# Fewer source columns picked by TensorE, more gathered by GpSimd, in the GAT passes of a graph network

## The chip, the cores and the metric

The kernel runs on one NeuronCore of a Trainium2 chip. The metric is device time in microseconds. The kernel before takes 10527.93 us, the median of 3 runs (10525.65 to 10530.43).

## The reference

A graph of 6250 nodes with 64 features and 100000 edges, sorted by destination, goes through four networks, each followed by a residual and a layer norm. What matters here is the second, a graph attention network (GAT) of five layers with one set of edges:

```python
h = x @ W
al = h @ a_src
ar = h @ a_dst
logit = leaky_relu(al[src] + ar[dst], 0.2)
alpha = segment_softmax(logit, dst)
out = segment_sum(alpha[:, None] * h[src], dst) + b
```

Four layers use W_std, then one uses W_skip on the concatenation of input and result. The first network sums rows by edge with a sigmoid weight, the third is again an attention with k[src] · q[dst] (in the kernel "dot"), the fourth has three layers with four heads ("multi").

## The kernel before, in words

The 100000 edges, padded, lie as 128 partitions × 784 columns, cut into CHUNKS = 28 chunks of K = 28 columns. A chunk is processed as a unit: the table rows of its 28 × 128 source nodes must stand in `rows[:, b]` (two buffers, b = chunk mod 2; the trace calls this memory `turned`), then DVE and ACT compute logits, running maxima and exponentials, DVE multiplies the rows with the weights (L1426) and scans them into sums by destination (L1446), and ACT turns the result (L1084, L1086) and stores it.

There are two ways to get a column of source rows (128 rows of 66 floats in GAT):

- **Gathered.** POOL issues one indirect DMA per column (L970). `gather` waits first for `rows_used[b]`, which DVE's L1426 of two chunks earlier signals.
- **Picked.** PE multiplies one-hot matrices with the table of all nodes, which is held on chip in `pair`, split in two parts of float32r. A column takes 7 sets × 2 parts = 14 matmuls of 462 columns (L1115). ACT makes the one-hots from keys (L733, L744), SP loads the keys. DVE takes each picked column out of its PSUM bank with a mask (L1236, `take`), and one reduction for half of the columns writes the rows (L1240).

`Picks.X` says how many of the 28 columns are picked: `COLS["gat"]` = 8 in four of the GAT edge passes and `FIRST_COLS` = 7 in the first; `KG = K - X` are gathered. EARLY = X // 2 columns of a chunk are taken ahead of the previous chunk's L1426, the rest after its scans. In the four passes with `ahead=2` the first chunk has further 2 × X columns picked, so that `gather(0, 0, KG - X * AH)` is short. The picked columns' PSUM banks form a ring of RING = 6 (`bank_of`).

Each engine runs its own program, and hardware loops (`Fori`) go over pairs of chunks; only semaphores order them, so the order is written out by hand. `layer` (L1891) does a node part (`nodes`) and the edge part (`edges`). `build` calls it once for the sum network with the first GAT edges, three times in a `Fori` for the standard layers, once for the last standard layer with W_skip edges, once for dot, and for the multi layers. PICKED = max(COLS.values()) sets how many key columns `prepare` computes and stores, and KEYS and KEY_TURNS follow from it.

The dot pass picks 4 of 28 columns with other code (L1128, L1222, L1227); the multi passes pick none.

Of the kernel before, what the change touches and what calls it, by code (L numbers as in the profile page):

```python
# [45 lines left out]
class Link:  # L46


    def __init__(self, eng, sem, base=0):
        self.eng, self.sem, self.base, self.n = eng, sem, base, 0  # L50
# [607 lines left out]
NG = 7  # L658
GC = C // NG
GROUPS = [(j * GC, (j + 1) * GC) for j in range(NG)]  # L660
COLS = {"gat": 8, "dot": 4}
FIRST_COLS = 7
PICKED = max(COLS.values())
HALF = D
KF = 2 * D
# [12 lines left out]
def edge_tiles(kind, update=False, clear=None, **_):  # L678

    X = COLS.get(kind, 0)  # L680
    multi_kind = kind == "multi"
# [18 lines left out]
class Picks:  # L700


    def __init__(self, nc, g, ph, kind, ahead, cols=None):
        X = self.X = cols or COLS[kind]
        self.ahead, self.first = ahead, AHEAD - ahead
# [1185 lines left out]
def layer(nc, g, node, edge=None):  # L1891

    with phase(nc) as ph:
        turned, rows = ph.shared("turned", *[f for f, _ in (node_tiles(**node), edge_tiles(**edge) if edge else ({}, {}))])
        wide, chunk = ph.shared("wide", *[f for _, f in (node_tiles(**node), edge_tiles(**edge) if edge else ({}, {}))])
        banks = ph.psum("banks", [P, 8, 512])[:]
        ph.now = ph.block()
        pk = Picks(nc, g, ph, edge["kind"], edge["ahead"], edge.get("cols")) if edge and edge["kind"] in COLS else None
        ready = nodes(nc, g, ph, banks, turned, wide, pk=pk, **node)
        if edge:  # L1900
            edges(nc, g, ph, banks, rows, chunk, ready, pk=pk, **edge)
# [6 lines left out]
def build(nc, a, out):  # L1908
    g = Graph()
    with ExitStack() as ctx:  # L1910
# [38 lines left out]
        with scratch(nc, "proj", [P, C, D + 2]) as proj:  # L1949
          g.proj = proj  # L1950
          with scratch(nc, "pair", [P, 2, SETS, D + 2, SET], F32R) as pair:
# [3 lines left out]
            std = dict(gat, weights=g.gat_w[0:D, 1, :])  # L1955
            layer(nc, g, dict(kind="sum", rows=g.x, w_o=a["l0_w"], **std), dict(kind="gat", ahead=0, cols=FIRST_COLS))
            with nc.Fori(0, 3):
# [86 lines left out]
```

## Time and profile before

| | us |
|---|---|
| timed, median of 3 runs | 10527.93 |
| profiled execution, its span | 14084.2 |
| gather loop of the first GAT pass | 1033.7 |
| gather loops of the four others | 1113.3, 1117.2, 1110.9, 1115.5 |
| gather loop of dot | 1220.1 |
| gather loops of multi | 1170.7, 1293.9, 1294.1 |
| POOL busy, DVE busy, PE busy | 7724.8, 7042.7, 6814.7 |

The profiled execution is one execution of the same program with the hardware profiler on; for it only the span is known, from the first to the last instruction, and no other time of its own. It is a third longer than the timed runs. In the tables of the profile PE is TensorE's matmuls, PEld its weight loads, DVE VectorE, ACT ScalarE, POOL GpSimd, SP SyncE. A "gather loop" is the stretch from the first to the last L970 of a layer. PEclk is the granted TensorE clock as a share of 2.4 GHz, so 0.50 is 1.2 GHz. "Issue" as the end of an idle time means that nothing shown in the profile was waited for.

### The profile page before, as it was taken

Reading aid. Unit: us, or ns where it says so; the run is one execution under the profiler, and the core shown is the slowest. Engines: PE = TensorE matmul, PEld = TensorE weight load, DVE = VectorE, ACT = ScalarE, POOL = GpSimd, SP = SyncE. Lnnn points to the kernel's source line nnn. Section 1 sums busy time; section 2 is a strip of 40 time slices with the busy share of each in tenths; the row PEclk is TensorE's granted clock in tenths of the full one; section 3 lists DMA queues with packets and bytes.
Section 4 is the critical chain, followed back from the end, with each engine's and each line's share of the span. In section 5 each row is a group of like instructions: output and inputs, shape, how many; then the busy total and the mean of one; then the engine's idle time right before and its main releaser. Section 6 shows DMA issues by size and latency. Waiting matters only on the chain. (4 is left out here: it accounts for less than half of the span.)

```text
span 14084.2 us, 100376 instructions
## 1 busy us (share of the span) xinstructions
PE 6814.7 (48%) x27637; PEld 5669.8 (40%) x27637; DVE 7042.7 (50%) x12322; ACT 5152.3 (37%) x5609; POOL 7724.8 (55%) x7576
## 2 busy tenths in 40 slices
PE   5443366657756774777577646661111322232222
PEld 5433355545545553655455535551111211121111
DVE  5333345434444443444444546663444466646666
ACT  0011144444434443444344424442222243423432
POOL 7888755544444445344444455546665555545553
PEclk7555577768777776887677767775555565556555
DMA  5333322212211221122133323333332344434442
GB/s 154 36 36 33 58 51 58 56 39 55 54 49 42 56 55 42 48 55 55 40 90 91 86 72 97 97 89 89 115 109 96 116 143 136 140 94 141 138 140 81
DMA packets 782270, 1137.56 MB, mean 81 GB/s; under 512 B 500471, under 2 KB 559955, under 8 KB 774499
## 3 DMA queue, kind: packets, MB, share of 16 engines
q0 software_dynamic: 355008, 370.44, 14.1%
q1 hardware_dynamic: 363245, 417.03, 9.6%
q10 hardware_dynamic: 63926, 349.09, 6.2%
q8 instruction: 32, 0.52, 0.0%
q14 instruction: 59, 0.48, 0.0%
HBM read 680.14 MB, written 468.70 MB: 82 GB/s over the span
## 5 line engine op out<-in xcount | busy, mean ns | idle before, releaser
L970 POOL DMA_INDIRECT turned<-d_t,idx x5788 | 5465.9, 944 | 5006.3 <-DVE wide L1426 3228.1
L1115 PE MATMUL banks<-pair,hot 128*128 128x462 f32 x16184 | 3981.1, 402 | 1677.0 <-issue 1661.2
L1115 PEld LDWEIGHTS banks<-pair,hot 128*128 128x128 f32 x16184 | 3357.4, 208 | 2299.7 <-issue 1921.1
L1236 DVE TENSOR_TENSOR wide<-banks,member 128x462 f32<-128x462 f32 x1156 | 689.9, 634 | 2788.3 <-remote 2123.6
L1084 ACT COPY wide<-wide 128x952 f32<-128x952 f32 (+2 forms) x252 | 503.4, 1997 | 2831.5 <-DVE wide L1446 2800.7
L650 POOL DMA_INDIRECT d_acc<-work,idx x784 | 1237.7, 1579 | 263.9 <-issue 234.4
L733 ACT ACTIVATE hot<-keys,row 128x1024 fp32r<-128x1024 f32 (+1 forms) x1036 | 1073.1, 1117 | 277.9 <-PE banks L1115 204.9
L1171 PE MATMUL banks<-ident,wide 128*128 128x128 f32 x588 | 163.1, 423 | 1814.2 <-issue 945.2
L1446 DVE TENSOR_TENSOR_SCAN wide<-banks,wide 128x224 f32<-128x224 f32 (+4 forms) x1288 | 1036.9, 871 | 5.8
L1128 PE MATMUL banks<-pair,hot 128*128 128x448 f32 x3136 | 804.7, 417 | 452.1 <-issue 393.8
L1128 PEld LDWEIGHTS banks<-pair,hot 128*128 128x128 f32 x3136 | 688.1, 221 | 568.7 <-issue 492.5
L744 ACT ACTIVATE hot<-hot 128x3584 fp32r<-128x3584 f32 (+1 forms) x296 | 905.2, 3105 | 0.6
L1171 PEld LDWEIGHTS banks<-ident,wide 128*128 128x128 f32 x588 | 103.5, 212 | 1881.9 <-issue 973.3
L1426 DVE TENSOR_TENSOR wide<-turned,banks 128x1792 f32<-128x1792 f32 x252 | 858.5, 3407 | 0.0
L1180 PE MATMUL banks<-wide,ident 128*128 128x512 f32 x224 | 199.5, 1026 | 1219.3 <-DVE wide L1319 1219.3
L1240 DVE TENSOR_REDUCE turned<-wide 128x264 f32<-128x1848 f32 (+1 forms) x296 | 601.6, 2033 | 10.1
L1180 PEld LDWEIGHTS banks<-wide,ident 128*128 128x128 f32 x224 | 63.0, 312 | 1303.0 <-issue 1303.0
L579 PE MATMUL banks<-ident,key_f 128*128 128x128 f32 x1568 | 248.9, 332 | 676.1 <-DVE key_f L528 645.1
L1294 DVE TENSOR_TENSOR_SCAN banks<-banks,wide 128x224 f32<-128x224 f32 x896 | 512.6, 618 | 117.7 <-DMA wide<-d_acc 70.4
L1086 ACT COPY wide<-wide 128x896 f32<-128x896 f32 (+2 forms) x252 | 521.2, 2068 | 48.3 <-remote 26.8
L1406 DVE SCALAR_TENSOR_TENSOR logits<-logits,we_rows 128x112 f32<-128x112 f32 x84 | 30.1, 358 | 1010.6 <-ACT we_rows L1000 944.6
L579 PEld LDWEIGHTS banks<-ident,key_f 128*128 128x128 f32 x1568 | 238.9, 240 | 685.6 <-DVE key_f L528 649.8
(311 smaller groups left out, 9556.1 us busy)
## 6 DMA issues: line engine op xcount, KB each, us to landing
d_e<-wide ACTq DMA_DIRECT2D x168, 924.0 KB
turned<-d_t,idx POOLq DMA_INDIRECT x5788
d_e<-wide ACTq DMA_DIRECT2D x84, 1008.0 KB
wide<-d_b SPq DMA_DIRECT2D x60, 1344.0 KB
keys<-d_key SPq DMA_DIRECT2D x124, 512.0 KB
d_b<-wide SPq DMA_DIRECT2D x28, 1344.0 KB
wide<-d_edge SPq DMA_DIRECT2D x84, 448.0 KB
d_em<-wide ACTq DMA_DIRECT2D x84, 448.0 KB
```

The source lines that it names most:

```text
L650: gp.indirect_dma_start(g.d_acc[r][:, :], offset(idx[:, b, k:k + 1]), sums[:, b, k, :], None, compute_op=ALU.add).then_inc(added[b][r], 16)
L733: last = nc.scalar.activation(pk.hot[:, place, :, j, :], pk.keys[:], ACT.Abs, bias=g.row[:, j * SET:j * SET + 1], scale=-1.0)
L744: last = nc.scalar.activation(part, part, ACT.Relu, bias=1.0, scale=-1.0)
L970: gp.indirect_dma_start(rows[:, b, k, :], None, table[:, :], offset(idx[:, b, k:k + 1])).then_inc(s["gathered"][b], 16)
L1086: nc.scalar.copy(state[:, :, FA:], values[:, b, FA:, :].rearrange("p f k -> p k f")).then_inc(s["states_turned"], 1)
L1115: mm = nc.tensor.matmul(ps_cols[i], hot[:, place, i, j, :], flat(g.pair[:, part, j]), start=(j, part) == (0, 0), stop=(j, part) == (SETS - ...
L1128: mm = nc.tensor.matmul(ps_cols[i][:, h], hot[:, i // 2, i % 2, j, :], flat(pk.pair[:, part, j, h * HALF:(h + 1) * HALF, :]), start=(j, pa ...
L1236: nc.vector.tensor_tensor(found[:, i - i0], ps_cols[i].rearrange("p (w c) -> p w c", c=SET), mid(member[:, i], TW), ALU.mult).then_inc(pic ...
L1240: link(nc.vector.tensor_reduce(rows[:, buf, at + i0:at + i1, :], found[:, 0:i1 - i0], AX.X, ALU.add))
L1294: last = nc.vector.tensor_tensor_scan(ps_q[:, f0 * K:(f0 + MR) * K], ps_same[:, 0:MR * K], flat(b_f[:, b, i * HEAD_ROWS + f0:i * HEAD_ROWS ...
L1426: nc.vector.tensor_tensor(V[:, 0:D, :].rearrange("p (h d) k -> p h d k", h=H), G[:, :, v0:v0 + D].rearrange("p k (h d) -> p h d k", h=H), ...
L1446: last = nc.vector.tensor_tensor_scan(flat(V[:, f0:f1, :]), flat(keep[:, m:m + f1 - f0, :]), flat(V[:, f0:f1, :]), 0.0, ALU.mult, ALU.add)
```

## The change

In the GAT passes TensorE picks 4 columns of a chunk in place of 8 (in the first pass in place of 7), and GpSimd gathers 24 in place of 20 (in place of 21). PICKED becomes 4, and everything that is derived from X follows.

```diff
-COLS = {"gat": 8, "dot": 4}
-FIRST_COLS = 7
+COLS = {"gat": 4, "dot": 4}
+FIRST_COLS = 4
 PICKED = max(COLS.values())
```

POOL in a layer with `ahead=2` (L1886 is the last DMA of the node part, the first L970 row the two gathers ahead of the loop, the second the loop body of two chunks):

```order
 L1886 DMA seed<-d_t,dst 128x66
 L961 UNCONDITIONAL_BRANCH
-L970 DMA turned<-d_t,idx 128x66 x24
+L970 DMA turned<-d_t,idx 128x66 x40
 L976 UNCONDITIONAL_BRANCH
 L976 ISA
-L970 DMA turned<-d_t,idx 128x66 x40
+L970 DMA turned<-d_t,idx 128x66 x48
 L976 REGISTER_ALU
```

Ahead of the loop 40 gathers stand in place of 24, and 48 in place of 40 in each pass of the loop.

DVE inside the loop, in the row that follows the logits (ISA rows are waits), where the early columns of the next chunk are taken ahead of L1425 and L1426:

```order
 L1232 ISA
-L1232 TENSOR_TENSOR member<-iota,in_set 128x56
-L55 REGISTER_ALU
-L1235 REGISTER_ALU
-L1236 TENSOR_TENSOR wide<-banks,member 128x462
...
-L1240 TENSOR_REDUCE turned<-wide 128x264
+L1232 TENSOR_TENSOR member<-iota,in_set 128x28
+L55 REGISTER_ALU
+L1235 REGISTER_ALU
+L1236 TENSOR_TENSOR wide<-banks,member 128x462
...
+L1240 TENSOR_REDUCE turned<-wide 128x132
 L55 REGISTER_ALU
```

Four takes and a reduction of 4 columns become two takes and a reduction of 2; the late columns change in the same way.

## Rows read from the trace of the kernel before

**Rows 1.** The page: span and instructions, busy time of each engine.
```profile
span 14084.2 us, 100376 instructions
PE 6814.7 (48%) x27637; PEld 5669.8 (40%) x27637; DVE 7042.7 (50%) x12322; ACT 5152.3 (37%) x5609; POOL 7724.8 (55%) x7576
```
**Rows 2.** Waits: who waited for whom: us in total, times, longest.
```profile
POOL turned L970 <- DVE wide L1426: 3228.1, 216, 83.1
DVE wide L1236 <- remote: 2123.6, 189, 37.1
...
DVE logits L1406 <- ACT we_rows L1000: 944.6, 74, 21.9
...
DVE wide L1236 <- PE banks L1115: 448.5, 199, 17.5
...
DVE proj L1222 <- remote: 315.6, 29, 46.1
```
**Rows 3.** Windows, gather loops: length, PE, PEld, DVE, ACT, POOL busy, PEclk, DMA, GB/s.
```profile
1774.90:2808.60 1033.70, 680.11 (x2708) 567.01 (x2708) 480.18 (x805) 467.68 (x419) 555.06 (x588) 0.78 0.22 56
2994.50:4107.80 1113.30, 792.41 (x3242) 669.52 (x3241) 527.50 (x851) 525.72 (x429) 513.43 (x544) 0.80 0.20 53
...
8240.20:9460.30 1220.10, 776.08 (x3021) 662.70 (x3020) 745.23 (x1123) 498.71 (x631) 634.44 (x672) 0.77 0.36 94
9657.70:10828.40 1170.70, 131.91 (x571) 122.61 (x571) 544.27 (x1143) 330.01 (x514) 740.22 (x784) 0.53 0.34 111
11050.60:12344.50 1293.90, 337.91 (x891) 204.46 (x891) 818.54 (x1522) 515.59 (x661) 741.08 (x784) 0.60 0.43 140
...
sum 10469.40, PE 5436.02 PEld 4442.23 DVE 5519.76 ACT 4428.77 POOL 5465.69; mean PE 604.00 PEld 493.58 DVE 613.31 ACT 492.09 POOL 607.30
```
**Rows 4.** Timeline, POOL: start, length, instruction, idle before and releaser.
```profile
4298.59 0.96 POOL L970 DMA_INDIRECT turned<-d_t,idx  x1 [0.31 <-issue]
...
4411.35 0.94 POOL L970 DMA_INDIRECT turned<-d_t,idx  x1 [83.10 <-DVE wide L1426]
...
4723.99 0.94 POOL L970 DMA_INDIRECT turned<-d_t,idx  x1 [0.30 <-issue]
...
4763.48 0.94 POOL L970 DMA_INDIRECT turned<-d_t,idx  x1 [16.08 <-DVE wide L1426]
```
**Rows 5.** Timeline, PE in the same steady chunk.
```profile
4713.15 23.39 PE L1115 MATMUL banks<-pair,hot 128*128 128x462 f32 x99 [0.85 <-issue]
4739.13 0.54 PE L1115 MATMUL banks<-pair,hot 128*128 128x462 f32 x1 [2.59 <-issue]
```
**Rows 6.** Timeline, PE at the start of a standard layer's loop.
```profile
4284.98 13.52 PE L1115 MATMUL banks<-pair,hot 128*128 128x462 f32 x55 [2.98 <-issue]
...
4318.54 0.54 PE L1115 MATMUL banks<-pair,hot 128*128 128x462 f32 x1 [2.95 <-issue]
...
4334.64 85.55 PE L1115 MATMUL banks<-pair,hot 128*128 128x462 f32 x397 [0.15 <-issue]
```
**Rows 7.** Timeline, DVE during the long run of rows 6.
```profile
4351.28 0.64 DVE L1236 TENSOR_TENSOR wide<-banks,member 128x462 f32<-128x462 f32 x1 [2.19 <-PE banks L1115]
4354.22 0.64 DVE L1236 TENSOR_TENSOR wide<-banks,member 128x462 f32<-128x462 f32 x1 [2.29 <-PE banks L1115]
...
4357.82 2.08 DVE L1240 TENSOR_REDUCE turned<-wide 128x264 f32<-128x1848 f32 x1
```
**Rows 8.** Groups of instructions: POOL's indirect DMAs outside the gather loops.
```profile
L650 POOL DMA_INDIRECT d_acc<-work,idx x784 | 1237.7, 1579 | 263.9 <-issue 234.4 <-ACT work L620 25.5 <-DMA d_acc<-work,idx 4.0
...
L1876 POOL DMA_INDIRECT wide<-d_e,idx_last x441 | 424.1, 962 | 145.1 <-issue 131.6 <-DMA d_e<-merged,idx_join 13.4
...
L1883 POOL DMA_INDIRECT d_b<-proj,idx_first x245 | 251.6, 1027 | 160.6 <-ACT proj L1820 89.8 <-issue 70.8
...
L1883 POOL DMA_INDIRECT d_b<-wide,idx_first x196 | 195.2, 996 | 186.1 <-ACT wide L1820 91.9 <-issue 53.7 <-ACT wide L1818 40.5
```
**Rows 9.** Timeline, PE after the last gather (4107.8) of a standard layer.
```profile
4111.46 16.27 PE L1115 MATMUL banks<-pair,hot 128*128 128x462 f32 x71 [0.86 <-issue]
```
**Rows 10.** Windows, as rows 3: a stretch at the lower clock, and the steady chunk.
```profile
4713.50:4718.00 4.50, 4.50 (x13) 3.85 (x13) 3.42 (x4) 0.00 (x0) 0.00 (x0) 0.50 0.00 0
4722.74:4763.48 40.74, 28.86 (x120) 24.59 (x119) 19.18 (x32) 18.26 (x15) 18.87 (x20) 0.79 0.19 53
```

## The prediction

> **What bounds the kernel now.** I read the page first [rows 1]. POOL is the busiest engine (55%), but no engine is near full, so shares settle nothing. The waits come next [rows 2]: POOL's gathers wait 3228.1 us in 216 waits for DVE's L1426, the multiply that gives a buffer of rows back, and DVE waits 2123.6 + 448.5 us at L1236 for the picked columns. So in this execution the chain is PE, then DVE, then POOL. The windows of the nine gather loops [rows 3] give the sizes: a standard GAT loop takes about 1115 us, of which POOL is busy 513.
>
> One steady chunk shows why. POOL issues 20 gathers, one every 1.248 us (0.944 busy, 0.30 between) [rows 4], then idles 16.08 us. This chunk takes 40.74 us [rows 10], and the 20 gathers fill 25 of them. PE's rows of the same chunk [rows 5] come in two kinds: 99 matmuls in 23.39 us, then single ones 2 to 3 us apart, with "issue" as the reason, so nothing that the profile shows holds them. At the start of a loop the pattern is plainer [rows 6]: single matmuls while POOL gathers, and 397 in 85.55 us once POOL is silent. A column is 14 matmuls; DVE takes one every 2.93 us there [rows 7], so eight columns need 23.5 us of PE and not 37 to 40.
>
> **How the profiled execution stands to the timed runs.** Its span is 14084.2 us, the median 10527.93: 3556 us less. Nothing in the kernel differs between the two. The largest thing that could shrink by as much is POOL's waiting: without the 3228.1 us the span is 10856. I conclude that PE's thin stretches belong mostly to the profiled execution. Then the timed run sits near a balance: 20 gathers of price p against 23.5 us of PE.
>
> What is p outside the profile? It lies between 0.944 (the gap gone) and 1.248 (all as shown). A balance over the whole program narrows it. Outside the nine loops lie 14084.2 − 10469.4 = 3615 us; 1666 other indirect DMAs stand there [rows 8] and get cheaper by (1.248 − p) each; about 100 us are late picks after the last gather (picks go on for 20 us after a standard loop, [rows 9]) and the like. That leaves 1436 + 1666p. The loops: first layer 588p + 7 (POOL sets it, since 7 columns are 20.5 us); four standard loops of 685 (worked out below); the first multi loop 784p + 10; the two later ones 28 × 36.2 each, their 46.2 a chunk [rows 3] less some 10 of the 12.8 us that L1406 waits on average for a product of the thin PE [rows 2]; dot 28 × 32.3, its 43.6 a chunk less the 315.6 / 28 us that L1222 waits [rows 2, 3]. The sum is 7126 + 3038p = 10528, so **p = 1.12**. The 7126 may be wrong by 200 us, which is ±0.07.
>
> **The change, part by part** (28 chunks a layer; the skip layer is built as the three standard ones, so four loops count alike).
> - *POOL.* A standard loop issues 24 × 28 − 8 = 664 gathers in place of 20 × 28 − 16 = 544, the first layer 672 in place of 588: 564 more in all.
> - *PE.* 56 matmuls a chunk in place of 112 (98 in the first layer): 11.7 us at full clock in place of 23.5. It is no longer near any limit.
> - *ACT and DVE.* The one-hot rows (L733, L744) halve, and of DVE's work four of eight takes of 0.64 us and half of two reductions of 2.08 go [rows 7]. Both engines had room within 25 us (DVE 19.2 and ACT 18.3 us busy in that chunk, [rows 10]), so this is costed at nothing; the cover is POOL's gathers, and if they did not cover it, it could only gain.
> - *Key loads and setup.* Half as many key bytes, one turned key tile less: a few us, counted as nothing, hidden behind POOL's scatters.
> - *Start of a loop.* Chunk 0 has 16 columns picked ahead and 4 gathered now; then 8 and 16. POOL's second burst is behind L1426 of chunk 0, and that is behind 28 picked columns (three groups of 8 and the early 4 of the next). PE starts 13.6 us before the first gather (4284.98 against 4298.59 [rows 4, 6]); 28 × 2.93 = 82, so 68 us after it; with the last take, reduction and L1426 75 us (shown: 112.8, with the thin stretch in it). After the change it is 14 columns, 41 us, released at about 35, while POOL has 40 gathers (45 us) to do: no wait.
>
> **Sum for a standard loop.** Before: release 0 at 75, one chunk every 23.5 us, release 25 at 663, last burst 20p: last gather ends at 685, and the last picks and last chunk take 20 more: 705. After: POOL never waits: 664p + 8 (0.3 us at each chunk) + 14 for the last chunk. With p = 1.12 this is 766: **+61 each, +243 for four.** First layer: 84p = **+94**. Together +337 us: 10528 + 337 = **10865**.
>
> The bounds of p: at 0.944 the same sum is 4 × (649 − 705) + 79 = −145, so 10383; at 1.248 POOL already sets the pace before (20 × 1.248 + 0.3 = 25.3 a chunk, 746 a loop) and it is 4 × (851 − 746) + 105 = +525, so 11053.
>
> After the change PE works less than half of a chunk, so its clock matters. The rows: at the lower level (0.50) 4.5 us hold 12 whole matmuls, 0.38 each [rows 10]; the long start-up run is at the upper one, 0.2155 each [rows 6]; and the granted clock is lowest, 0.53, in the loop where PE works least, the first multi loop [rows 3]. 56 matmuls at 0.38 are 21 us, below the 26.9 of 24 gathers: no cost. The Trainium skill, "TensorE: Matmul & The Clock Gate", section "HAM oscillation — how this bites in real kernels", says that PE falls back to half rate when it idles between bursts, so that every burst starts slow. By that rule a start-up's 14 columns take 75 us, not 41, of which POOL's 40 gathers cover all but some 23: the sum would be +337 + 92 = +429. The rows show that burst at full clock after a dozen matmuls, so I keep +337.
>
> **The rivals.**
> - *POOL's price is the full 1.248.* For it: the gap of 0.30 between gathers [rows 4] recurs unchanged and looks like the engine's own. Against: then the timed runs must have lost over 400 us outside the loops that no row shows as idle. Time 11053. Its harshest form puts every added gather on the path, at each loop's start too: 564 × 1.248 = +704, 11232. Against that stand the 83.10 us that POOL waits there now [rows 4] and that shrink, so it gets 2 in 100 by itself. The Trainium skill, "Perfetto Trace Analysis", section "Identifying the Most-Contended Engine", has the rule behind it: relieve the engine with the highest occupancy first, and here that engine is given more.
> - *Faster: PE's thin stretches are partly real.* If the timed PE also loses time while POOL gathers, a chunk before is longer than 23.5 us, and the balance above lowers p to match. With p = 1.00 the balance leaves 365 us, 2.2 a chunk over the 168 picking chunks (28 in each of five GAT layers and dot): a standard loop was 763 and becomes 686, the first layer +84 − 60, together −284: 10244. It decides where the old loop's loss outweighs the dearer POOL: at p about 1.06, with 1.1 us lost a chunk. For it: the stretches follow POOL's bursts to within some us, as contention would. Against: to lose much, POOL must be much cheaper than shown, and its 0.944 of busy time is a floor.
> - *The two effects cancel* (p near 1.06): 10528.
> - That the change does not do what it says is ruled out by the order of the instructions.
>
> **How the numbers follow.** Forecast (p 1.07 to 1.19, PE clean): 0.54. Full price, its harshest form included: 0.19. Faster: 0.21. Cancelling: 0.06. A measurement here can tell 0.2% (21 us) from no change, so slower 0.73, same 0.06, faster 0.21. The time is the likeliest case's, 10865. The range runs from 10390 (the lower bound of p; it leaves out half of the faster rival) to 11055 (the upper bound).
>
> **What the changed profile would show.** L970 ×6352 in place of 5788; L1115 ×8288. In the GAT layers POOL's wait for L1426 all but gone, one unbroken row of gathers 1.248 apart, PEclk lower. Since those waits vanish, the *profiled* GAT loops get shorter (664 × 1.248 + 8 = 837 in place of about 1115, first layer 847 in place of 1033.7), and the profiled span falls by some 1200 to 1300 us although the timed median rises. Dot and multi loops unchanged. The forecast is wrong if the median falls with the span, or if POOL still waits in the standard loops.

## The result

The change takes 11179.81 us, the median of 4 runs (11175.43 to 11182.93), against 10528.74 for the kernel before (4 runs, 10525.65 to 10530.43). The ratio is 1.0617 (95% interval 1.0602 to 1.0632): slower by 651 us, 6.2%. Forecast were 10865 and a range up to 11055. The direction was right, and the loss is nearly twice the one forecast.

Quote of the page of the changed kernel, its span and busy times and two of its groups; they answer to [rows 1]:

```profile
span 11178.5 us, 83592 instructions
PE 4839.5 (43%) x19740; PEld 4043.7 (36%) x19740; DVE 6426.9 (57%) x11757; ACT 4316.5 (39%) x5609; POOL 8268.3 (74%) x8140
...
L970 POOL DMA_INDIRECT turned<-d_t,idx x6352 | 5999.7, 945 | 1945.7 <-issue 1930.5
L1115 PE MATMUL banks<-pair,hot 128*128 128x462 f32 x8288 | 2081.6, 417 | 2107.6 <-ACT hot L744 2033.9
```

The first thing to see is the span: 11178.5 us, 1.3 us below the timed median. The profile of before had a span of 14084.2 beside timed runs of 10528. This was taken for a property of the profiled execution; the experiments find it on two chips in timed runs too, so it is most likely one of the chip that the profile was taken on (no record says which one that was). POOL is now busy for 74% of the span, and the rest of its time at L970 is 1930.5 us in 6328 steps of 0.30 us with no one to wait for.

The waits of the changed kernel (who waited for whom: us in total, times, longest), to be read beside [rows 2]:

```profile
DVE idx L1356 <- DMA turned<-d_t,idx: 2454.3, 187, 27.0
PEld banks L1115 <- issue: 2085.4, 130, 16.7
PE banks L1115 <- ACT hot L744: 2033.9, 130, 16.3
POOL turned L970 <- issue: 1930.5, 6328, 0.7
```

POOL's wait for DVE's L1426 has fallen from 3228.1 to 15.2 us in all. DVE now waits for gathered rows (L1356), and PE for its one-hots, which come at the pace of the chunks. Everything is behind POOL.

Windows of the changed kernel (length, PE, PEld, DVE, ACT and POOL busy, PEclk, DMA share, GB/s): the gather loops of the first GAT pass, two standard layers, dot and two multi layers, beside [rows 3]:

```profile
1764.10:2602.80 838.70, 388.81 (x1557) 332.38 (x1555) 402.23 (x737) 349.07 (x416) 634.19 (x672) 0.73 0.28 67
2759.10:3587.90 828.80, 378.34 (x1484) 322.86 (x1484) 400.44 (x734) 344.34 (x411) 626.68 (x664) 0.72 0.29 67
3745.40:4574.20 828.80, 378.92 (x1484) 323.51 (x1484) 400.49 (x734) 344.38 (x411) 626.74 (x664) 0.72 0.29 67
6709.30:7558.20 848.90, 682.47 (x3034) 614.53 (x3033) 753.50 (x1134) 502.39 (x635) 634.39 (x672) 0.88 0.51 135
7733.10:8711.70 978.60, 133.40 (x588) 124.13 (x588) 555.88 (x1170) 339.42 (x532) 739.94 (x784) 0.55 0.42 135
8876.00:9856.80 980.80, 348.99 (x893) 206.16 (x894) 830.67 (x1544) 524.60 (x676) 742.21 (x784) 0.64 0.58 185
```

Divide a length by its number of gathers: 838.7 / 672 = 1.248, 828.8 / 664 = 1.248, 978.6 / 784 = 1.248, 980.8 / 784 = 1.251. POOL's rhythm is the length of every loop. The dot and multi loops, whose code the change does not touch, take 849, 979 and 981 us here and took 1220, 1171 and 1294 in [rows 3]. That alone says that the profile of before is not of the same kind of execution.

PE at the start of a standard loop and in a steady chunk of the changed kernel (start, length, instruction, idle before), beside [rows 5, 6]:

```profile
3695.91 44.31 PE L1115 MATMUL banks<-pair,hot 128*128 128x462 f32 x196 [3.02 <-DVE pair L767]
...
4102.41 14.63 PE L1115 MATMUL banks<-pair,hot 128*128 128x462 f32 x56 [15.67 <-ACT hot L744]
```

There are no single matmuls any more. The 14 columns of the start (196 matmuls) are done in 44.31 us, before POOL's first gather at 3745.37. PE starts 49.5 us ahead of that gather, and not 13.6 as in [rows 4, 6].

### The profile page after: what moved, and what is told of

Read it like the earlier page. It is cut to its first block and busy times, and to the rows that moved or that the text cites. A ratio compares the mean times of both kernels' runs of the same rounds, so it can differ in the third digit from the quotient of the medians.

```text
span 11178.5 us, 83592 instructions
## 1 busy us (share of the span) xinstructions
PE 4839.5 (43%) x19740; PEld 4043.7 (36%) x19740; DVE 6426.9 (57%) x11757; ACT 4316.5 (39%) x5609; POOL 8268.3 (74%) x8140
## 5 line engine op out<-in xcount | busy, mean ns | idle before, releaser
L970 POOL DMA_INDIRECT turned<-d_t,idx x6352 | 5999.7, 945 | 1945.7 <-issue 1930.5
L1115 PE MATMUL banks<-pair,hot 128*128 128x462 f32 x8288 | 2081.6, 417 | 2107.6 <-ACT hot L744 2033.9
L1115 PEld LDWEIGHTS banks<-pair,hot 128*128 128x128 f32 x8288 | 1782.1, 218 | 2406.0 <-issue 2085.4
L1356 DVE COPY idx<-src 128x28 int32 x252 | 47.1, 187 | 2459.7 <-DMA turned<-d_t,idx 2454.3
L1426 DVE TENSOR_TENSOR wide<-turned,banks 128x1792 f32<-128x1792 f32 x252 | 853.3, 3386 | 0.0
L1063 ACT ACTIVATE banks<-factors 128x28 f32<-128x28 f32 (+1 forms) x252 | 55.7, 221 | 1928.7 <-DVE factors L1416 1928.7
L1128 PE MATMUL banks<-pair,hot 128*128 128x448 f32 x3136 | 705.7, 390 | 171.2 <-ACT hot L759 166.4
L1128 PEld LDWEIGHTS banks<-pair,hot 128*128 128x128 f32 x3136 | 635.6, 204 | 241.4 <-issue 172.0
L733 ACT ACTIVATE hot<-keys,row 128x512 fp32r<-128x512 f32 x1036 | 651.4, 710 | 104.2 <-ACT wide L1086 43.2
L1876 POOL DMA_INDIRECT wide<-d_e,idx_last x441 | 438.0, 993 | 145.1 <-issue 131.6
L620 ACT COPY work<-banks 128x512 f32<-128x512 f32 x112 | 51.5, 546 | 1228.9 <-DMA d_acc<-work,idx 1217.3
L744 ACT ACTIVATE hot<-hot 128x1792 fp32r<-128x1792 f32 x296 | 483.9, 1681 | 0.6
L1017 ACT COPY wide<-wide 128x28 f32<-128x28 f32 (+2 forms) x240 | 418.1, 1742 | 159.1 <-DMA wide<-d_b 110.9
```

The lines of the kernel that those rows point to most:

```text
L733: last = nc.scalar.activation(pk.hot[:, place, :, j, :], pk.keys[:], ACT.Abs, bias=g.row[:, j * SET:j * SET + 1], scale=-1.0)
L744: last = nc.scalar.activation(part, part, ACT.Relu, bias=1.0, scale=-1.0)
L970: gp.indirect_dma_start(rows[:, b, k, :], None, table[:, :], offset(idx[:, b, k:k + 1])).then_inc(s["gathered"][b], 16)
L1115: mm = nc.tensor.matmul(ps_cols[i], hot[:, place, i, j, :], flat(g.pair[:, part, j]), start=(j, part) == (0, 0), stop=(j, part) == (SETS - ...
L1128: mm = nc.tensor.matmul(ps_cols[i][:, h], hot[:, i // 2, i % 2, j, :], flat(pk.pair[:, part, j, h * HALF:(h + 1) * HALF, :]), start=(j, pa ...
L1426: nc.vector.tensor_tensor(V[:, 0:D, :].rearrange("p (h d) k -> p h d k", h=H), G[:, :, v0:v0 + D].rearrange("p k (h d) -> p h d k", h=H), ...
```

## Experiments

Theories: **A**, POOL issues a gather every 1.248 us in timed runs too and paces every loop, the only other cost being a short wait at the start of each standard loop; **B**, the prediction's price of 1.12; **C**, the profiler stretches PE.

### The kernel before once more, and three parts of the change

e_before is the kernel before, unchanged.

> The kernel before, unchanged, profiled once more, since the changed kernel's profile spans no more than its timed runs. Theory A (POOL sets the pace in undisturbed runs, each gather costs the full 1.248 us, and the earlier profile was a disturbed execution): a span near 10528 us, gathers 1.248 us apart, PE without thin stretches, the four standard GAT gather loops near 690 us each and the last multi loops near 980 us as in the changed kernel. Theory B (the price of 1.12 from the prediction): gathers about 1.12 us apart, standard loops near 685 us. Theory C (the profiler always thins out PE in this kernel): a span near 14084 us again.

It took 10534.89 us, with a span of 10533.0. Its page, two windows (first pass, a standard loop) and two more (both kinds of multi loop):

```profile
span 10533.0 us, 100376 instructions
PE 6226.2 (59%) x27637; PEld 5319.9 (51%) x27637; DVE 7031.4 (67%) x12322; ACT 5148.8 (49%) x5609; POOL 7742.1 (74%) x7576
...
L970 POOL DMA_INDIRECT turned<-d_t,idx x5788 | 5467.8, 945 | 1824.4 <-issue 1751.4
```

```profile
1765.90:2502.50 736.60, 616.38 (x2741) 529.70 (x2739) 491.49 (x821) 470.06 (x420) 555.05 (x588) 0.96 0.32 80
2660.40:3352.30 691.90, 664.56 (x3138) 587.46 (x3136) 525.92 (x852) 511.88 (x420) 513.62 (x544) 0.99 0.33 85
...
7087.70:8066.40 978.70, 132.93 (x588) 123.84 (x588) 555.83 (x1170) 339.20 (x532) 740.06 (x784) 0.55 0.42 135
8230.60:9210.80 980.20, 346.63 (x892) 205.26 (x893) 829.48 (x1543) 523.75 (x676) 741.73 (x784) 0.63 0.58 185
```

This is a profile of the kind that the timed runs are of. PE runs at 0.99 of its clock in a standard loop and is busy 664.56 of 691.9 us; POOL's gathers are still 1.248 apart. A standard loop is 544 × 1.248 = 679 us and a wait of 13. Where the wait comes from is seen in the timeline of the same kernel: PE at the start of a loop (the row goes on to the end of the stretch asked for, 3625) and in a steady chunk of the loop before, DVE's first multiply, then POOL:

```profile
3460.97 164.20 PE L1115 MATMUL banks<-pair,hot 128*128 128x462 f32 x771 [3.02 <-DVE pair L767]
```

```profile
2996.56 23.93 PE L1115 MATMUL banks<-pair,hot 128*128 128x462 f32 x112 [1.00 <-DVE wide L1236]
```

```profile
3548.69 3.56 DVE L1426 TENSOR_TENSOR wide<-turned,banks 128x1792 f32<-128x1792 f32 x1
```

```profile
3510.46 0.96 POOL L970 DMA_INDIRECT turned<-d_t,idx  x1 [0.30 <-issue]
...
3539.20 0.94 POOL L970 DMA_INDIRECT turned<-d_t,idx  x1 [0.30 <-issue]
3553.07 0.94 POOL L970 DMA_INDIRECT turned<-d_t,idx  x1 [12.93 <-DVE wide L1426]
```

PE starts 49.5 us ahead of the first gather and goes through without a pause. 28 columns at 2.93 us are 82 us, so they are picked at 3543; with the last takes, the reduction and the multiply itself, L1426 of chunk 0 ends at 3552.3. POOL's 24 gathers end at 3540.1, so it waits 12.93 us. The prediction had PE only 13.6 us ahead [rows 4, 6]. In the steady chunk PE's 112 matmuls take 24.0 us and then PE waits 1 us for DVE: it could go on 4% faster than POOL's 20 gathers, 25.0 us, let it.

**e_pool**: PE picks as before, POOL issues the change's number of indirect DMAs.

```diff
+            for k in range(EX if columns == KG else EX0):
+                gp.indirect_dma_start(spare_rows[:, b, k, :], None, table.rearrange("n (w o) -> (n w) o", o=1),
+                                      offset(idx[:, b, k:k + 1])).then_inc(s["gathered"][b], 16)
...
```

The lines left out (...) set how many are added, and let those who wait for the gathers wait for the added ones too.

> Only POOL's part of the change: PE still picks 8 (7) columns, POOL issues 4 (3) more indirect DMAs per chunk, of one word per partition into spare words that nobody reads, 12 more in the first burst of the layers that pick ahead, so that it issues as many as the changed kernel. Theory A: 11180 us, up to 11280 if POOL still waits 25 us at each loop's start. Theory B: the price of POOL alone gives 10865 us and the rest of the changed kernel's loss comes from PE, so near 10865.

11183.56 us, ratio 1.0619 (1.0588 to 1.065); the same edit again, on another chip, r_pool2, gave 11178.99, ratio 1.0619 (1.0603 to 1.0635). POOL's extra issues alone give the whole loss, with PE, ACT and DVE as they were. The group of the added ones:

```profile
L977 POOL DMA_INDIRECT spare_rows<-d_t,idx x564 | 532.4, 944 | 171.9 <-issue 171.9
```

944 ns each and 0.305 between, with 4 bytes a row in place of 264: the price of a gather here is one of the instruction and not of its bytes.

**e_std4**: the change in the four later passes only (the first keeps 7 columns; some columns of chunk 0 take other nodes' rows).

```diff
-COLS = {"gat": 8, "dot": 4}
+COLS = {"gat": 4, "dot": 4}
-PICKED = max(COLS.values())
+PICKED = max(*COLS.values(), FIRST_COLS)
...
```

> The change in the four later GAT passes only; the first pass keeps its 7 picked columns. Theory A: 84 gathers fewer than the changed kernel at 1.248 us, 105 us less: 11075 us. Theory B: 94 us less by price but the first pass has no start-up of picks, so 11040 to 11090: this run alone does not tell A from B, it says whether the parts add up.

11071.18 us, ratio 1.0513 (1.0482 to 1.0543). The first pass is worth the remaining 108.6 us, against 84 × 1.248 = 105. The parts add up within 4 us (the two times are of different sets of runs, whose kernels before differ by 2 us).

**e_halfpe**: the same columns with half of PE's work (the low part of the table's values is left out).

```diff
-                    for part in range(2):
+                    for part in range(1):
...
```

> The kernel before, with the low part of each table value left out of the picked columns: 7 matmuls a column in place of 14 (the output is less exact). Theory A: PE costs only where POOL waits at a loop's start, so at most 60 us faster, 10470 to 10525. Theory B: standard loops are paced by PE at 23.5 us a chunk and fall to 20 x 1.12 us, some 200 us faster in all, near 10300.

10482.64 us, ratio 0.9955 (0.9936 to 0.9975). The standard loops fall from 692 to 679 us, which is 544 × 1.248; 4 × 13 is 52, and 48 were measured. Half of PE's matmuls are worth the four start-up waits and nothing else: in a steady chunk PE's 24.0 us lie below POOL's 25.0.

### Other sizes, on a second kind of chip

The next runs, together on one chip, were e_gat6 (6 picked columns everywhere in GAT), e_first8 (8 in the first pass too), e_ahead1 (`ahead=1` in the four later passes) and the kernel before for its profile.

```diff
-COLS = {"gat": 8, "dot": 4}
-FIRST_COLS = 7
+COLS = {"gat": 6, "dot": 4}
+FIRST_COLS = 6
```

```diff
-FIRST_COLS = 7
+FIRST_COLS = 8
...
+    if summing:
+        del tiles["agg"]
...
-    agg = g.h if lent else tiles["agg"]
+    agg = g.h if lent or summing else tiles["agg"]
...
```

The second edit is that of e_first8: its node part keeps its sums in memory that is free there, which makes room for the eighth column (two statements that use the sums are reshaped for it).

> Half way between the two kernels: 6 picked columns in the GAT passes (4 in the change, 8 before), 6 in the first. Standard loops have 22 x 28 - 12 = 604 gathers, the first 616. Theory A (POOL issues one gather every 1.248 us and paces every loop; the only other cost is the wait at the start of a standard loop, 13 us at 8 columns): at 6 columns the first multiply needs 21 picked columns, 62 us, and PE starts 41 us ahead of POOL, so POOL's 32 gathers (40 us) cover it and no wait is left. Standard loops 754 us (692 before), first 769 (737): 4 x 62 + 32 = +280, 10815. Theory B (the price of 1.12 of the prediction): first +31, standard loops 604 x 1.12 + 22 - 705 = -6 each, about 10540. Theory D (the loss is in proportion to the gathers added, 268 of 564, without a wait that goes first): +309, 10844, with loops at 761.

> The other way: 8 picked columns in the first GAT pass too (its node part keeps its sums in the free half of xh, which makes the room). 28 gathers fewer. Theory A: the first loop goes from 737 to 702 us, since PE's 23.5 us a chunk still lie below POOL's 25.0: -35, 10499. Theory B (1.12): PE would pace at 23.5 in place of 21 x 1.12 = 23.5: no change. Theory E (with ahead=0 the first pass has PE and POOL starting together, so 8 columns make PE late once): a wait of some us at the loop's start, first loop 702 to 715.

> 8 columns as before, but 8 of chunk 0's columns picked ahead in place of 16 in the four later passes: 552 gathers in place of 544 a loop. Theory A: PE's burst ahead of the first multiply is 20 columns in place of 28, 59 us in place of 82, so it ends before POOL is through its 32 gathers (40 us after PE's lead of 41) and the wait of 13 us goes; the loop is 552 x 1.248 = 689 in place of 692: -3 each, about 10522. Theory F (the 13 us wait is set by something else than the number of columns ahead): the wait stays and the loops are 702: +40, 10574.

> The kernel before once more, for its profile alone. Theory A (the first profile of before, 14084 us, was of one disturbed execution): span about 10533 again, waits of POOL for L1426 about 73 us in all. Theory C (the profiler stretches PE in some part of its executions): a span well above 10600 and thin stretches of PE in it.

None of the times came, because the kernel before itself took 13903.58 us here (16 runs, 13885.54 to 13922.14), profiled span 13910.0. Its loops (1033.1 us, then 1085, and 1205 for dot) are within 3% of those of [rows 3]: the execution that the prediction read, now seen in timed runs. The profile looks as theory C wants it (a long span, thin stretches of PE), but timed and profiled time are the same here, 13904 and 13910, so theory C is wrong as well. It is not the profiler; **there are chips on which this kernel takes a third longer**, and the first profile of before most likely came from one. On this one the ratios were small: 6 columns gave 0.998 (0.9971 to 0.999), 8 in the first pass 1.0031 (1.0019 to 1.0044), and `ahead=1` 0.9957 (0.9943 to 0.997).

The same three and the change were run again, and these runs fell on a chip of the first kind (before 10531.88).

> The change itself, once more, to see it on whichever kind of chip comes up. If the kernel before takes about 10530 us here: theory A gives 11180 again, loops of 839 and 829 us. If it takes about 13900 us here (a chip on which PE's matmuls come singly, 2 to 3 us apart, while POOL gathers): theory G (there a chunk's length is set by PE's slow stretches and not by POOL, and 4 or 6 or 8 columns end within 2% of each other, as 6 columns did) gives standard loops of 1060 to 1110 us, and 13750 to 13950 in all. Theory H (the time on such a chip follows PE's number of matmuls, 56 in place of 112 a chunk) gives loops below 950 and a time below 13300.

> 6 picked columns, once more. If before takes about 10530 us here, theory A: standard loops 754, first loop 769, no wait of POOL, 10815; theory D (in proportion, 268 of 564 gathers): 10844; theory B (price 1.12): about 10540. If before takes about 13900: a ratio of 0.998 again.

> 8 picked columns in the first pass too, once more. If before takes about 10530 us here, theory A: first loop 702 in place of 737, 10499, ratio 0.9967; theory B: no change; theory E: first loop 705 to 715. If before takes about 13900: 1.003 again, first loop 1059 in place of 1033.

> 8 of chunk 0's columns picked ahead in place of 16, once more. If before takes about 10530 us here, theory A: loops of 689 in place of 692, 10522; theory F: the wait of 13 us stays, loops 702, 10574. If before takes about 13900: 0.996 again.

| | theory A | measured | ratio, interval |
|---|---|---|---|
| the change | 11180 | 11180.12 | 1.0617, 1.0599 to 1.0634 |
| 6 columns | 10815 | 10809.34 | 1.0266, 1.0249 to 1.0283 |
| 8 in the first pass | 10499 | 10496.12 | 0.9967, 0.9956 to 0.9979 |
| `ahead=1` | 10522 | 10523.59 | 0.9992, 0.9983 to 1.0002 |

Windows, 6 columns, first pass and a standard loop:

```profile
1763.40:2532.20 768.80, 549.88 (x2345) 482.06 (x2343) 461.09 (x793) 433.12 (x420) 581.39 (x616) 0.85 0.30 75
2688.90:3442.80 753.90, 543.10 (x2298) 473.26 (x2296) 457.92 (x789) 422.36 (x411) 570.15 (x604) 0.85 0.31 76
```

The first pass with 8 columns, and a standard loop with `ahead=1`:

```profile
1763.30:2462.30 699.00, 668.05 (x3136) 588.34 (x3136) 522.39 (x849) 511.08 (x420) 528.65 (x560) 0.99 0.33 85
```

```profile
2659.60:3348.60 689.00, 646.07 (x3024) 563.92 (x3022) 516.76 (x844) 498.05 (x411) 521.05 (x552) 0.99 0.33 85
```

Each loop is its number of gathers times 1.248, at four sizes: 604 give 753.9, 616 give 768.8, 560 give 699.0, 552 give 689.0. The 699.0 leaves no room for theory E's wait. With `ahead=1` PE's burst is 20 columns, 59 us, of which 49.5 lie ahead of the first gather (the expectation reckoned with 41; both are enough), so it ends in time and the wait goes, at the price of 8 gathers, 10 us: 13 are traded for 10. Its ratio alone can't be told from 1; the loop's length, 689.0 for 691.9, shows it. With proportion instead of a wait that goes first (theory D, 10844) 6 columns would have come out 35 us higher than they did.

### The change on the second kind of chip, and both small gains together

> The change once more. If before takes about 10530 us on this chip: 11180 (theory A). If it takes about 13900: theory G (PE's slow stretches beside POOL's gathers set a chunk's length, whatever the number of columns) gives standard loops of 1060 to 1110 us and 13750 to 13950 in all; theory H (the time follows PE's number of matmuls) gives loops below 950 and less than 13300.

> Both small changes together: 8 columns in the first pass, and 8 columns picked ahead in place of 16 in the later ones. If before takes about 10530 us here, theory A: -35 and -9 to -12, about 10486, ratio 0.9956. If before takes about 13900: the two measured ratios, 1.003 and 0.996, multiply to 0.999.

> Half of PE's matmuls for each picked column (the low part of the table's values is left out), POOL and DVE as before. If before takes about 10530 us here: 10483 again, ratio 0.9955. If before takes about 13900: theory G gives 0.97 to 1.00; theory H, by which the number of matmuls counts there, gives standard loops below 950 and a ratio below 0.96.

> The kernel before, for its profile beside r_halfpe2 on the same chip. If its time is about 10530: waits of POOL for L1426 near 73 us in all and loops of 692, as in e_before. If about 13900: waits above 3000 us and loops near 1085, as in e_before2.

These runs fell on another chip of the second kind (before 14058.6 us in 15 runs). **There the change is faster**: 13879.63 us, ratio 0.9872 (0.9857 to 0.9887). Half of PE's work gives 13536.15, ratio 0.9627 (0.9612 to 0.9641), and both small gains 0.9992 (0.9983 to 1.0001). First pass and a standard loop of before there, of the change, and the standard loop with half of PE's work:

```profile
1777.80:2816.60 1038.80, 677.34 (x2706) 562.93 (x2706) 480.85 (x805) 467.08 (x418) 555.28 (x588) 0.77 0.20 56
3002.70:4117.20 1114.50, 793.52 (x3246) 671.55 (x3246) 528.81 (x852) 525.37 (x429) 513.74 (x544) 0.80 0.18 53
```

```profile
1778.40:2819.90 1041.50, 462.35 (x1531) 350.25 (x1529) 389.29 (x708) 341.90 (x413) 634.19 (x672) 0.65 0.20 53
3007.40:4064.90 1057.50, 477.82 (x1604) 362.75 (x1603) 399.15 (x721) 350.26 (x423) 626.58 (x664) 0.66 0.20 52
```

```profile
2964.70:3967.60 1002.90, 465.23 (x1633) 368.38 (x1631) 534.68 (x861) 521.29 (x429) 513.32 (x544) 0.70 0.20 59
```

The 3002.70 and 3007.40 rows make the comparison: the loop is 57 us shorter (the three other standard loops 50 to 53), the four together 209, the dot loop, whose code is the same, 15, and the first pass gives 3 back. That is 221 of the 227 us between the two profiled spans (14077.9 and 13850.8); the medians are 179 apart, since the profiled run of the change was the fastest of its four by 26 us and that of before is 21 above its median. 57 is the balance of two large terms. With PE's matmuls halved and the gathers as before the loop falls by 112; the change issues as few matmuls (56 a chunk) and is 55 above that, for 120 gathers that would take 150 us if each lengthened the loop. The waits of the change there, and PE beside a chunk's gathers:

```profile
PEld banks L1115 <- issue: 3331.3, 1462, 10.6
PE banks L1115 <- issue: 2740.7, 1351, 10.4
DVE wide L1236 <- remote: 2700.2, 138, 37.8
POOL turned L970 <- DVE wide L1426: 2336.4, 159, 49.0
```

```profile
4754.23 0.54 PE L1115 MATMUL banks<-pair,hot 128*128 128x462 f32 x1 [2.43 <-issue]
4757.04 0.55 PE L1115 MATMUL banks<-pair,hot 128*128 128x462 f32 x1 [2.27 <-issue]
4759.82 0.54 PE L1115 MATMUL banks<-pair,hot 128*128 128x462 f32 x1 [2.24 <-issue]
```

The single matmuls are here with 4 columns too, 1351 of them waiting for nothing that is shown. POOL still waits 2336.4 us for L1426, where e_before3 has 3215.5, so its added gathers fall partly into idle time, and PE's lighter load counts. The expectation of the loops (1060 to 1110 under theory G) was just missed at 1057.5 (the four run from 1055.5 to 1062.3), and the time lay within its 13750 to 13950; but the same theory allowed half of PE's work no more than 3% and it gave 3.7%, while theory H wanted loops below 950. Neither is right: PE's number of matmuls counts there, but for less than H would have it.

The last runs, on a chip of the first kind again:

> Both small changes together once more. If before takes about 10530 us on this chip, theory A: -35 and -9 to -12, about 10486, ratio 0.9956. If before takes 13900 to 14060: 0.999 again.

> PE as before, POOL with the change's number of indirect DMAs (the added ones of one word into spare words). If before takes about 10530 us here: 11183 again, ratio 1.062. If it takes 13900 to 14060: PE's matmuls come singly while POOL gathers, so every added gather of 1.248 us should delay PE too, and PE's full-speed part is as long as before: the loops grow by about 5 us a chunk, as much as POOL's time does, +650 us in all and a ratio of 1.046; if POOL's added time fell into its idle time of 3000 us there, the ratio would be 1.00.

r_pool2 is reported above. r_best2 took 10483.7 us, ratio 0.9957 (0.9943 to 0.9971), where 10486 was expected. It has 8 columns in the first pass and `ahead=1` in the others, computes the whole reference, and is faster than both kernels, by 0.4% and 6.2%. On the second kind of chip it can't be told from before.

## Why the prediction was wrong in size

- **The failed step is the price of a gather, which explains 188 of the 314 us that were missed** (its own sum gives +525 at 1.248, +337 at 1.12), under "What is p outside the profile?": p = 1.12 was inferred, and 1.248 is what the rows showed and what timed runs have. The balance behind it took the whole profile, less POOL's waits, as that of the timed runs, and asked what price would close the gap. Its constant, 7126, was said to be good to 200 us. At 1.248 it would have to be 10528 − 3038 × 1.248 = 6737, so it was off by 389. In e_before the excess is found: outside the loops 3243 us (10533.0 less the nine loops' 7290), where the balance at 1.248 has 1436 + 1666 × 1.248 = 3515; the two later multi loops 1961 in place of 2027; dot 846 in place of 904. These make 396. The chip of the first profile needs 372 us more outside the loops (3615 against 3243), of which the balance took off 100, and about 1 us a chunk more in the two later multi loops and 2 in dot than it took off.
- **The premise above it** ("thin stretches of PE belong to the profiled execution") was half right. They are absent from the timed runs of the first kind, so the conclusion for PE held: 24.0 us a chunk, beside 23.5 forecast. They belong to the chip and not to the profiler, so that chip's timed runs have them.
- **POOL.** The counts held: 564 more gathers. As priced by the rows they are 704 us. *The second failed term is the start of a loop*: the first multiply was to come 75 us after the first gather against a burst of 30, so that the change would win 45 us a loop back. PE's lead is 49.5 us and not 13.6, the multiply ends at 42 us, and 13 us a loop are won back: 704 − 4 × 13 = 652, and 651 were measured. The 13.6 was read rightly, but it too is of the other kind of chip: the lead is 49 us in all standard loops of e_before and 10 to 13 in those of e_before3. This term makes the other 126 us of the miss: 45 forecast and 13 measured are 32 a loop. The rival "harshest form", 11232, which was given 2 in 100, was the nearest; what spoke against it, the wait of 83.10 us, was of the other kind of chip.
- **The full-price bound**, 11053, fell short by the same start-up term (4 × 32 = 128 us; 127 by the times). The range's upper end rested on it. Its 0.3 us at each chunk (8 us a loop) is not there either, 664 × 1.248 being the whole 828.8, but it stood in both kernels and cancelled.
- **PE, ACT and DVE at nothing** held: e_pool gives 11183.56 with none of their work taken away.
- **The lower clock** held as costed at nothing on this kind: in the changed loops it is 0.72, 56 matmuls take 14.63 us of a chunk of 30, and the start-up's 196 take 44.31, all done before POOL's first gather. The half-rate start that the Trainium skill describes ("TensorE: Matmul & The Clock Gate", section "HAM oscillation — how this bites in real kernels") reached no gather of POOL's. The prediction priced it at half rate for the whole burst, 75 us and +429; the trace agrees with a slow start but it is a small one, 2 us (44.31 against 42.2 at 0.2155 each), so that +429 lay nearer to 651 than +337 is luck.
- **The most-contended engine.** The rule of the Trainium skill ("Perfetto Trace Analysis", section "Identifying the Most-Contended Engine"), that the highest occupancy is relieved first, was weighed lightly because POOL's 55% did not look like a bound. In the profile of the timed kind POOL has 74%, and the trace agrees with the rule: 6 columns +2.7%, 4 columns +6.2%, 8 in the first pass −0.3%.
- **The faster rival** (10244) is wrong on this kind. Its mechanism, PE losing time while POOL gathers, is real on the other, where the change does win 1.3%.
- **The changed profile.** L970 ×6352, L1115 ×8288, next to no wait for L1426 and loops of 838.7 and 828.8 (forecast 847 and 837) came as said. A span of about 12,800 did not: dot, multi and the node parts changed too, which the forecast excluded.

## What to carry to other kernels

If the span of a profile is a third above the timed median, do not repair it with a balance: a loop that the question does not touch (here multi, 784 gathers at 1.248 = 978 us at the least) shows how far the rest is stretched, and prices that repeat to a few ns (0.944 + 0.30) are to be kept. Then give the change's added instructions on the busiest queue their full price and take off only waits whose two sides are both known. An edit that shifts work between two engines within 4% of each other (25.0 against 24.0 us) loses the full price of the dearer one as soon as that sets the pace. And where two kinds of chip are in use, time on both: the sign can differ.

## What the runs showed of the hardware

- **Two kinds of chips.** The median of the kernel before was 10528 to 10532 us in four sets of runs, on at least three chips, and 13904 and 14059 on two others, where the runs of one chip spread over 0.3%. The change is 6.2% slower on the one and 1.3% faster on the other. No chip came up in two sets of runs, so whether a chip keeps its kind, or was in a passing condition that lasted through its set, is not shown.
- **The second kind is not slower everywhere.** Windows of e_before and e_before3 from the first scatter to the first gather:

```profile
176.50:1765.90 1589.40, 631.42 (x3266) 608.26 (x3267) 573.43 (x809) 197.79 (x232) 1294.33 (x836) 0.56 0.37 41
```

```profile
189.30:1777.80 1588.50, 631.03 (x3306) 607.38 (x3305) 580.82 (x818) 198.01 (x232) 1293.46 (x836) 0.57 0.35 40
```

  1589.4 and 1588.5 us, with nearly the same clock. An indirect DMA has the same 945 ns and 0.30 on both. Nearly all of the time is lost from the first GAT loop on: e_before3 less e_before is 302 us in that loop, 1674 in the four standard ones, 379 in dot, 810 in the three multi loops and 379 outside the loops, of which 12 ahead of the first. In the GAT loops it shows as single matmuls with "issue" ahead of them beside POOL's gathers: 1665.7 us at L1115 in e_before3, where in e_before L1115 waits 187.4 us for everything together. That is not the whole of it, since the multi loops pick nothing and lose time too. What holds PE's instructions back there, and what lengthens multi, stays open: no run varied it by itself, and r_pool2, meant to show whether more gathers lengthen a chunk there, fell on the first kind.
- **A gather's price on POOL does not depend on its bytes**: 944 ns at 4 bytes a row and 945 at 264, and the gap of 0.30 is paid in timed runs as in the profile, at all four sizes of loop above. Other indirect DMAs cost more, as the scatter of [rows 8] with 1579 ns.
